# Four attention layers on one core: loads in order of use, the first projections ahead of the set-up products, and new turn tables for the opening and the end

## The reference

```
layer 0: x1 = x + gamma_sa * w_o . attention(theta(x), phi(x), g(x))        # 32 latent channels
         x1 = x1 + gamma_moca * w_o . attention(theta(x1), concepts, concepts)
layer 1: x2 = x1 + gamma * attention(Wq x1 + bq, Wk x1 + bk, Wv x1 + bv)     # q, k of 32 channels, v of 256
layer 2: h = group_norm(x2); x3 = x2 + proj . attention(q(h), k(h), v(h))    # one head of 256 channels
layer 3: h = group_norm(x3); c = 8 heads of 32 channels, attention(q(h), k(h), v(h))
         out = layer_norm(c . wo + bo) + x3
```

## Time and profile before

| what | us |
|---|---|
| median of 3 runs | 2710.54 |
| the profiled execution | 2716.84 |
| its span in the trace | 2715.0 |
| PE busy | 2536.3 (93%) |
| DVE busy | 1870.5 (69%) |
| ACT busy | 1281.9 (47%) |
| POOL busy | 591.2 (22%) |

### The profile page before, as it was taken

The page is one execution under the profiler, slowest core; times in us unless marked ns, Lnnn a source line. Parts: engine busy times, 40 slices in busy tenths (PEclk is TensorE's granted clock), DMA queues, the critical chain, the costliest instruction groups (busy, mean ns, idle before and its releaser), DMA issues.

```text
span 2715.0 us, 26577 instructions
## 1 busy us (share of the span) xinstructions
PE 2536.3 (93%) x9892; PEld 1431.6 (53%) x9892; DVE 1870.5 (69%) x1925; ACT 1281.9 (47%) x2209; POOL 591.2 (22%) x322
## 2 busy tenths in 40 slices
PE   7989989999999999999999999999999999988887
PEld 4466654464654656455564646546564555544432
DVE  5544327787487865787677874878657876769995
ACT  2453221646346562555526464364625555135466
POOL 0083130050110502023010401105010130124463
PEclk8999996999999899999999999998999999978898
DMA  2000002020302003020120203010030201222201
GB/s 76 1 0 1 1 17 62 1 47 16 93 1 47 1 24 86 1 47 1 62 47 1 47 1 109 1 39 9 16 93 1 47 1 47 47 62 47 47 16 47
DMA packets 33777, 88.93 MB, mean 33 GB/s; under 512 B 10608, under 2 KB 10800, under 8 KB 33392
## 3 DMA queue, kind: packets, MB, share of 16 engines
q1 hardware_dynamic: 33648, 87.23, 12.0%
HBM read 19.79 MB, written 16.78 MB: 13 GB/s over the span
## 4 chain that ended last, share of the span: by engine, by line
PE 75%; DVE 15%; ACT 4%; issue 3%; POOL 2%; SPq 1%; DMA 1%; DVEq 0%; ACTq 0%; POOLq 0%
PE ps L654 11%; PE ps L687 10%; PE ps L673 9%; PE ps L805 8%; PE ps L974 7%; PE ps L896 6%; PE ps L662 6%; PE ps L809 4%; DVE ba_nmx L1358 2%; PE ps L743 2%; PE ps L882 2%; DVE fa_nmx L1358 2%; DVE accb L1527 2%; DVE bb_nmx L1358 1%; DVE w L1527 1%
## 5 line engine op out<-in xcount | busy, mean ns | idle before, releaser
L1358 DVE TENSOR_REDUCE ba_nmx<-ps 128x1 f32<-128x1024 f32 x448 | 531.3, 1219 | 115.9 <-PE ps L673 114.1
L1211 ACT ACTIVATE prb<-ps 128x512 f32<-128x512 f32 x896 | 483.9, 604 | 220.4 <-PE ps L687 215.5
L1527 DVE TENSOR_TENSOR accb<-accb,prb 128x1024 f32<-128x1024 f32 x312 | 396.1, 1303 | 78.0 <-ACT prb L1211 77.1
L687 PE MATMUL ps<-qs,ks 97*128 97x512 f32 x896 | 349.4, 479 | 20.9 <-DMA qs<-ba_nmx_r 16.3
L1069 ACT ACTIVATE pr<-ps 128x512 f32<-128x512 f32 x336 | 198.2, 604 | 334.8 <-PE ps L896 260.4
L673 PE MATMUL ps<-ks,qs 96*128 96x512 f32 x896 | 333.3, 471 | 17.7 <-DVE ba_nmx L1358 15.8
L576 POOL TENSOR_TENSOR q2k<-pr,q2k 128x512 fp32r<-128x512 f32 x112 | 147.7, 1338 | 797.5 <-ACT q2k L1106 797.5
L687 PEld LDWEIGHTS ps<-qs,ks 97*128 97x128 f32 x896 | 170.5, 203 | 215.2 <-issue 101.7
L673 PEld LDWEIGHTS ps<-ks,qs 96*128 96x128 f32 x896 | 175.3, 206 | 122.5 <-DVE ba_nmx L1358 51.4
L974 PE MATMUL ps<-prb,vb 128*32 128x512 f32 x1792 | 230.0, 633 | 0.2 <-ACT prb L1211 0.2
L1358 DVE TENSOR_REDUCE fa_nmx<-ps 128x1 f32<-128x1024 f32 x168 | 198.0, 1216 | 34.1 <-PE ps L882 18.9
(11 more groups left out here) (329 smaller groups left out, 3528.7 us busy)
## 6 DMA issues: line engine op xcount, KB each, us to landing
qs<-part SPq DMA_DIRECT2D x168, 128.0 KB, 2.5
ks<-part SPq DMA_DIRECT2D x168, 128.0 KB, 2.5
xm<-in_x SPq DMA_DIRECT2D x8, 1024.0 KB, 4.8
kept<-xm SPq DMA_DIRECT2D x8, 1024.0 KB, 4.2
prb<-kept SPq DMA_DIRECT2D x14, 512.0 KB, 3.7
out<-prb SPq DMA_DIRECT2D x28, 256.0 KB, 2.0
q2k<-part SPq DMA_DIRECT2D x48, 128.0 KB, 2.4
w<-in_weights SPq DMA_DIRECT2D x1, 2592.0 KB, 8.8
```

The lines of the kernel that those rows point to most:

```text
L687: return pe.matmul(o.ps[:, bank, :], keys[0:ROW + 1, tile(jt)], queries[0:ROW + 1, cols(ic)], start=True, stop=True)
L1211: act.activation(weights3(o, n, g), o.ps[:, turn3[score_use(s, g) % 3], :], ACT.Exp)\
L1358: dve.tensor_reduce(o.nmx[:, head, it:it + 1], o.ps[:, bank:bank + 2, :], AX.XY, ALU.max, negate=True).then_inc(o.max_sb[n].sem, 1)
L1527: dve.tensor_tensor(o.sums[pair], o.pairs[(now - 1) % RING][pair] if j == 1 else o.sums[pair], o.pairs[now % RING][pair], ALU.add).then_in ...
```

## The change

1. SP issues the columns `qk0` of `w` first, then image 0, then the other columns of `w`, and behind them `cst`, `vec`, `wo_con`, `con1` and image 1.
2. DVE scales `qk0` as soon as these columns are there (`loaded_first`, then `setup_theta_phi`), and fills the two rows of ones before it waits for the rest. `setup_dve` counts to 15.
3. `batches` takes `lead` steps of front 0 ahead of a function `setup`: PE makes both projection steps of image 0 ahead of the set-up products, ACT its four copies out of PSUM ahead of its wait for the set-up. DVE's set-up stays wholly ahead of its steps.
4. The set-up products use PSUM banks 4 to 7 instead of 0 to 6, since image 0's projections stand in banks 0 and 1. Their number and shapes are the same.
5. The tables `ORDER` of "fronts" and "backs" are new on PE, ACT, DVE and POOL, that of "backs" on SP too. Those of "both" are unchanged.

```diff
-SETUP_DVE = 16
+SETUP_DVE = 15
 ...
     ("fronts", "POOL"): (
-        14, 2, 3, 3, 2, 1, 5, 18, 6, 1, 1, 3, 1, 2, 1, 2,),
+        15, 1, 1, 1, 1, 3, 5, 1, 2, 18, 5, 1, 2, 4, 1, 1, 1, 2,),
 ...
-def batches(engine, front, back):
+def batches(engine, front, back, lead=0, setup=None):
 
     last = [back(b) for b in range(B)]
-    finish(merged("fronts", engine, front(0), chain(front(1), head(last[0]))))
+    first = front(0)
+    for _ in range(lead):
+        next(first)
+    if setup:
+        setup()
+    finish(merged("fronts", engine, first, chain(front(1), head(last[0]))))
 ...
         def _(sp):
-            sp.dma_start(w[:], weights.rearrange("(h p) n -> p h n", p=P)).then_inc(loaded.sem, 16)
+            w_v = weights.rearrange("(h p) n -> p h n", p=P)
+            first = W_COLS["qk0"]
+            sp.dma_start(w[:, :, first], w_v[:, :, first]).then_inc(loaded_first.sem, 16)
+            sp.dma_start(xm[0][:], x_v[0]).then_inc(x_loaded[0].sem, 16)
+            sp.dma_start(w[:, :, first.stop:], w_v[:, :, first.stop:]).then_inc(loaded.sem, 16)
+            sp.dma_start(cst[:], constants).then_inc(loaded.sem, 16)
             sp.dma_start(vec[:], vectors).then_inc(loaded.sem, 16)
             sp.dma_start(wo_con[:], small).then_inc(loaded.sem, 16)
             sp.dma_start(con1[:, L:2 * L], concepts).then_inc(loaded.sem, 16)
-            sp.dma_start(cst[:], constants).then_inc(loaded.sem, 16)
-
-            for b in range(2):
+
+            for b in range(1, 2):
                 sp.dma_start(xm[b][:], x_v[b]).then_inc(x_loaded[b].sem, 16)
 ...
         def _(pe):
-            pe.wait_ge(loaded.sem, 16 * 5)
             pe.wait_ge(setup_pool.sem, 6)
+            pe.wait_ge(loaded_first.sem, 16)
+            pe.wait_ge(setup_theta_phi.sem, 1)
+
+            def setup():
+                pe.wait_ge(loaded.sem, 16 * 5)
 ...
+                pe.wait_ge(setup_dve.sem, SETUP_DVE)
 ...
-            batches("PE", lambda b: program(front_of(b))[0](b), lambda b: program(back_of(b))[1](b))
+            batches("PE", lambda b: program(front_of(b))[0](b), lambda b: program(back_of(b))[1](b), 2, setup)
 ...
         def _(act):
             act.preload_act_table_set("natural_log_exp_and_others")
-            act.wait_ge(loaded.sem, 16 * 5)
             act.wait_ge(setup_pool.sem, 6)
-            act.wait_ge(setup_dve.sem, SETUP_DVE)
+
+            def setup():
+                act.wait_ge(loaded.sem, 16 * 5)
+                act.wait_ge(setup_dve.sem, SETUP_DVE)
 ...
-            batches("ACT", lambda b: program(front_of(b))[0](b), lambda b: program(back_of(b))[1](b))
+            batches("ACT", lambda b: program(front_of(b))[0](b), lambda b: program(back_of(b))[1](b), 4, setup)
 ...
         def _(dve):
+            dve.wait_ge(loaded_first.sem, 16)
+            dve.tensor_scalar(w[:, :, W_COLS["qk0"]], w[:, :, W_COLS["qk0"]], C ** -0.5, None, ALU.mult)\
+                .then_inc(setup_theta_phi.sem, 1)
+            for o in fronts:
+                dve.memset(bf32(o.ks01[ROW:ROW + 1, :]), 1.0).then_inc(setup_dve.sem, 1)
+
             dve.wait_ge(loaded.sem, 16 * 5)
             dve.tensor_copy(ident_r[:], ident).then_inc(setup_dve.sem, 1)
-            for o in fronts:
-                dve.memset(bf32(o.ks01[ROW:ROW + 1, :]), 1.0).then_inc(setup_dve.sem, 1)
 ...
-            scale(w[:, :, W_COLS["qk0"]], C ** -0.5)
             scale(w[:, :, W_COLS["q2"]], C ** -0.5)
```

78 lines of the change are left out of this document (40 added, 38 removed), and 34 rows, old and new, of the table ORDER.

## The result

| what | before | after |
|---|---|---|
| median, us | 2711.86 (2708.70 to 2719.36, 4 runs) | 2685.27 (2683.04 to 2686.21, 4 runs) |
| ratio, with its 95% interval | 1 | 0.9897 (0.9875 to 0.9919) |
| the profiled execution | 2716.84 | 2686.13 |
| its span | 2715.0 | 2684.3 |

The changed kernel is 26.6 us faster, 1.0%.

The account below looks back on a forecast made before the run. PE, busy for 93% of the span, was taken as the bound, leaving only its standing time. Gains of 4.0 + 1.0 + 2.2 + 4.7 = 11.9 us gave 2699 us, with an 8-in-10 range of 2687 to 2710.

Parts of the forecast that it names:

- Loads: Opening: `qk0` lands at 3.1 us, image 0 at 6.0, PE begins at about 6.2 instead of 21.84.
- rival of shared DMA engines: Opening: image 0 shares them with the weights, lands at about 8.5, opening wins nothing; 7.9 us gain, 2703; chance 0.13.
- First projections: Opening on PE: image 0's passes end at 10.7 to 13.0 us; image 1's take about 5.6, to 29.9.
- Set-up: Opening on PE: parameters at 13.9 us, set-up products still take 10.2, ending at 24.1 instead of 21.6.
- DVE and the sum of the opening: Image 0's three DVE operations run under image 1's projections; reductions end at 45.0; opening gains 4.0 us, bounds 1.0 to 5.5.
- The same distances as before up to 2373: Sign of being right: after the opening, the trace keeps its earlier distances until "backs" begins.
- Start of "backs": Image 6's projection step moves into PE's 7.25 us wait for image 7's group norm; gain 1.0 us, bounds 0 and 1.9.
- Total of image 6 and sums of image 7: End: PE starts image 6's total 2.2 us earlier; layer-norm operations moved behind image 7's sums save DVE 4.7 us.
- The rest of the tables: Other turns in "fronts" and "backs": taken at nothing; bounds 10.5 us of gain, 13.6 us of loss.
- Everything comes: Rival: opening at its most, most of the 6.79 stall and all 7.65 us; 20 us gain, 2690.5; chance 0.15.
- A wrong turn of POOL: Rival: POOL's new opening turns cost PE one more 13.6 us wait; 1.7 us slower, 2712; chance 0.07.
- The end is not DVE's: Rival: ACT and PE feed the last sums, so both end terms vanish; 5.0 us gain, 2705.5; chance 0.15.

Follow-up runs that it names:

- three fillings: The changed kernel with 3 matmuls nobody reads on PE ahead of its wait for the second shift rows of images 0 to 5; 2681.0 us, ratio 0.9882.
- end old: The changed kernel with all five tables of "backs" as before; 2704.4 us, ratio 0.9968 to the kernel before.

## Why the prediction was wrong

- **Loads.** Right: `qk0` at 2.97 (3.1), image 0 used at 6.71 (6.2; 6.3 to 7.4 in the eighteen executions with the new loads), parameters at 14.32 (13.9). The rival of shared DMA engines (8.5) is out. The fit beside it in the working is given in the Trainium skill, "DMA: Bandwidth & Descriptors", section "Anatomy of one DMA — SWDGE (gpsimd) path", for DMAs that GpSimd issues, and image 0 is issued by SP; no sum used it.
- **First projections.** Right: end of image 0's at 12.88, within 10.7 to 13.0; image 1's took 5.40 (5.6).
- **Set-up.** Mis-sized: 7.1 us where I carried over 10.2. Image 1's projections therefore ended at 27.1, not 29.9. The cause is the granted clock, not the change: the same products took 5.5 us at 1.00 and 8.5 at 0.61. Before, the views print 1.00 for the set-up, but the first level on record in that trace is at 25.7 us, and the durations speak for the lower level ahead of it: the small products took 1.87 us, and the projections' passes stand 0.85 us apart up to 25.4 and 0.43 from 25.97 on. So the 10.2 that I carried over was the set-up at its slowest, and that image 1's projections beat my 29.9 by 2.8 us is the clock's chance and not the change's doing.

```profile
25.97 0.19 PEld L654 LDWEIGHTS ps<-xm,w 128*128 128x128 f32 x1 [0.24 <-issue]
26.40 0.19 PEld L654 LDWEIGHTS ps<-xm,w 128*128 128x128 f32 x1 [0.24 <-issue]
```

- **DVE and the sum of the opening.** Reduction at 43.2 (45.0), `fa` at 57.2 (59.5), gain 4.6 to 7.5 by the medians against my 4.0 (at most 5.5), too near to it to call the term refuted. The mechanism, image 0's three operations under image 1's projections, is what the trace shows. But I credited it to loads and leads, and these alone measured 0: it needs the new tables of "fronts". With DVE's alone the time was lost again by 334 us.
- **"The same distances as before up to 2373".** Nearly: from `fa`'s first cast to "backs" 2307.6 us against 2309.7.
- **Start of "backs".** The quarter won 2.4 to 3.8 and not 1.0, and not by the step that I named: without it the end was 318.5. The passes that were to run faster take 3.76 us for four as before.
- **Total of image 6 and sums of image 7.** 2.2 + 4.7 = 6.9 forecast, 4.3 to 5.7 measured. PE's wait went from 6.79 to 3.08, near the 4 that I had named, but not because DVE's sum had become the last: DVE's ends at 2616.2 and POOL's at 2618.4. The "issue" ahead of the last total is POOL too, which my working had not as a candidate. The layer norm of image 6 was cheaper behind the sums, as forecast: 0.68 to 0.75 us for an operation once POOL was through, against up to 2.90, and the tail did not grow.
- **The rest of the tables.** This is the step that failed: "I take at nothing: an engine waits somewhere else instead". What the runs showed in its place: the end's tables win 19 to 22 us where I had 7.9. Its second and third quarters alone gave 8.4 + 5.2 us by the two profiled executions, 7.3 to 8.6 against the two other old ends, and 14 to 18 when undone. Two things were at work that my working did not have. DVE is busy for 12.6 to 13.6 us less in the end, and fewer of its sums run long beside POOL's; I had priced only moved operations and waits. And the old order lets PE's clock fall in the second quarter in one execution of three. In these quarters PE had stood still for 77.0 - 67.87 = 9.1 and 52.0 - 46.61 = 5.4 us and DVE for 10.5 and 2.3, and I had not read them. The bound for a gain, 10.5, came from a stretch of the opening, where nothing changed: the earlier trace rows and the stretch of 150 to 200 after are alike.
- **Rivals.** "Everything comes" was nearest with 2690.5 and was still short, for the same reason. "A wrong turn of POOL": its longest wait rose from 13.6 to 14.8 and its old table makes no difference. "The end is not DVE's" had 2705.5, and the quarter whose terms it struck out measured 4.3 to 5.7.

With the undone quarters put in, the sum is 21.1 and 4.6 to 7.5, so 25.7 to 28.6 us against 26.6 measured.

## What to carry to other kernels

- A merge of two streams written as tables is priced stretch by stretch. For each stretch whose tables change, read how long the engines of each pair stand still for each other, and how many of DVE's operations run beside POOL's: an order can also change how long the same instructions take. "Another wait takes its place" is no default.
- Before explaining the distance of two traces in a stretch, look at the same stretch in a second execution of the same order. Here 5.7 of 8.4 us in one quarter, and 5.4 us of the cast in the opening, came and went with the granted clock.
- An early load or an early step is worth something only if the next engine's order takes it first.
- Tables of several engines are one object: a part taken from PE or from DVE alone cost more (17.0 and 15.7 us) than the same part taken from both (12.2). Undo such changes by stretches, not by engines.

## What the runs showed of the hardware

- The granted clock falls behind waits of PE of 2.7 us and comes back: at 0.50 in 1244 to 1248, at 1.00 in the same place when the wait is filled. The Trainium skill, "TensorE: Matmul & The Clock Gate", section "HAM oscillation — how this bites in real kernels", says that waiting between bursts makes the clock fall again and that one pays for it in every round. The rows agree on the fall. On the price they differ by place: behind these waits, where DVE had 4.00 of 4 us, three fillings gave back 4.3 us by the medians, with overlapping intervals; in the second quarter of the old end the same order took 77.1 us at 0.86 and 71.4 at 0.95.
- PE's durations follow the record of the clock: eight small products take 1.87 us at 0.50 (20.55 in "end old") and 1.05 at 1.00 (20.39 after). A row over several us hides this: the changed kernel's set-up reads 0.76, but consists of 0.50 in 16 to 18 and 1.00 in 20.4 to 21.4. Where a trace has no level on record yet, as before up to 25.7 us, the views print 1.00.
- POOL and DVE side by side: a sum on DVE took 3.2 us in 2641 to 2658, with POOL's sums end to end beside it, and 1.21 at 2640.21, as in the earlier trace rows. DVE is busy for 270.5 to 271.5 us in three old ends and 257.9 to 258.3 in seven new ones, with 213 instructions in each; the order decides how many of its sums run long beside POOL's (32 or 25 of 56).

```profile
16.00:18.00 2.00, 2.00 (x5) 1.60 (x6) 1.93 (x6) 1.10 (x2) 0.00 (x0) 0.50 0.01 2
```

```profile
20.40:21.40 1.00, 1.00 (x9) 0.96 (x8) 0.61 (x3) 0.00 (x0) 0.00 (x0) 1.00 0.00 0
```
